# A mixture-of-experts kernel: 54 bf16 products that nothing reads are put into TensorE's stream between the last attention product and the expert stage

## What is computed

```python
# q = layernorm(x), k = v = ctx; four heads of 128
D = exp(log_D - max_log_D)                # decay from the cumulated forget gates, lower triangle
C = (q @ k.T / sqrt(dh)) * D
h = (C / (max(|C.sum|, exp(-max_log_D)) + eps)) @ v
x = x + tanh(g_xattn) * headnorm(h) * (1 + ln_weight)
xf = layernorm(x)                         # 4096 tokens
topw, topi = top_k(softmax(xf @ Wg.T), 2) # two of eight experts
# each expert takes its first CAP rows, in order of token, first choices first
y = gelu(rows @ W1[e] + b1[e]) @ W2[e] + b2[e]
x = x + tanh(g_ffn) * sum(topw * y of the two experts)
```

## Time and profile before

| | |
|---|---|
| median of 3 runs | 1940.94 us |
| lowest, highest | 1933.74, 1941.27 us |
| the profiled execution | 1937.9 us |
| its span | 1936.1 us |
| TensorE busy | 1823.9 us, 94% of the span |
| VectorE, ScalarE, GpSimd busy | 66%, 57%, 36% |
| mean granted clock of TensorE | 0.969 of full |

### The profile page before, as it was taken

How to read it: one execution, slowest core, us unless ns; L and a number is a source line. 1 busy time by engine, 2 the same in 40 slices (tenths; PEclk the granted TensorE clock), 3 DMA queues, 4 the chain that set the end, 5 groups by cost and what they waited for, 6 DMA issues and landing times.

```text
span 1936.1 us, 34120 instructions
## 1 busy us (share of the span) xinstructions
PE 1823.9 (94%) x11068; PEld 1579.1 (82%) x11068; DVE 1276.4 (66%) x2881; ACT 1107.3 (57%) x2035; POOL 688.5 (36%) x506
## 2 busy tenths in 40 slices
PE   4989977679999999999999999999999999999997
PEld 3776756578888888888888888888888888888886
DVE  3589987676667665766576657665766576657651
ACT  3567767665556555646555555555555555556543
POOL 0000110225443544354435443534354335333333
PEclk9899997589999999999999999999999999999999
DMA  5246453506554655465546555655465545554544
GB/s 172 88 170 223 152 175 109 146 18 125 105 108 92 124 99 113 90 118 99 116 86 121 99 113 93 116 99 116 91 116 96 116 94 113 98 114 90 95 72 58
DMA packets 177814, 214.77 MB, mean 111 GB/s; under 512 B 20464, under 2 KB 102512, under 8 KB 176608
## 3 DMA queue, kind: packets, MB, share of 16 engines
q0 software_dynamic: 50176, 90.77, 31.9%
q1 hardware_dynamic: 127456, 121.74, 20.1%
HBM read 123.10 MB, written 89.34 MB: 110 GB/s over the span
## 4 chain that ended last, share of the span: by engine, by line
PE 81%; DVE 7%; issue 4%; ACT 3%; DMA 2%; SPq 1%; another core or an unknown queue 0%; POOL 0%; DVEq 0%; POOLq 0%; ACTq 0%
PE PS L999 39%; PE PS L977 32%; PE PS L824 3%; DMA vs<-in_ctx_dram 2%; PE PS L815 2%; PE PS L955 2%; PE PS L763 1%; DVE x_lo L1725 1%; PE PS L888 1%; ACT heads L1110 1%; PE PS L843 1%; SPq L455 1%; DVE stats L1388 1%; DVE c_top L1746 1%; PE PS L777 1%
## 5 line engine op out<-in xcount | busy, mean ns | idle before, releaser
L677 POOL DMA_INDIRECT out_dram<-y_out,rows_now x288 | 487.5, 1693 | 828.2 <-ACT y_out L1306 687.2
L977 PE MATMUL PS<-x_hi,w_hi 128*128 128x270 f32 x1792 | 521.7, 291 | 15.0 <-issue 5.8
L977 PE MATMUL PS<-x_lo,w_hi 128*128 128x270 f32 x1792 | 517.5, 289 | 0.0
L977 PE MATMUL PS<-x_hi,w_lo 128*128 128x270 f32 x1792 | 517.1, 289 | 0.0
L999 PE MATMUL PS<-w_hi,h_hi 128*120 128x512 f32 x1152 | 458.2, 398 | 7.9 <-DVE h_lo L1732 7.9
L999 PE MATMUL PS<-w_lo,h_hi 128*120 128x512 f32 x1152 | 453.8, 394 | 0.0
L999 PE MATMUL PS<-w_hi,h_lo 128*120 128x512 f32 x1152 | 453.2, 393 | 0.0
L977 PEld LDWEIGHTS PS<-x_hi,w_hi 128*128 128x128 f32 x1792 | 340.4, 190 | 42.4 <-issue 11.8
L977 PEld LDWEIGHTS PS<-x_lo,w_hi 128*128 128x128 f32 x1792 | 341.2, 190 | 20.8
L977 PEld LDWEIGHTS PS<-x_hi,w_lo 128*128 128x128 f32 x1792 | 340.0, 190 | 0.0
L999 PEld LDWEIGHTS PS<-w_hi,h_lo 128*120 128x120 f32 x1152 | 208.9, 181 | 58.7
(11 more groups left out here) (192 smaller groups left out, 2298.6 us busy)
## 6 DMA issues: line engine op xcount, KB each, us to landing
w_raw<-in_L_ffn_W_dram SPq DMA_DIRECT2D x128, 256.0 KB, 3.8
w_raw<-in_L_ffn_W_dram SPq DMA_DIRECT2D x64, 512.0 KB
x_front<-in_x_dram SPq DMA_DIRECT2D x8, 1024.0 KB, 7.0
vs<-in_ctx_dram SPq DMA_DIRECT2D x32, 256.0 KB, 4.7
maxima<-maxima_rows SPq DMA_DIRECT2D x8, 1024.0 KB, 4.8
x_back<-in_x_dram SPq DMA_DIRECT2D x8, 1024.0 KB, 8.8
out_dram<-x_back SPq DMA_DIRECT2D x8, 1024.0 KB, 6.7
xn_rows<-xn SPq DMA_DIRECT2D x8, 1024.0 KB, 9.4
```

Of the source, the lines that this page charges most:

```text
L677: G.indirect_dma_start(out=out[:, :], out_offset=bass.IndirectOffsetOnAxis(ap=rows_now[0:RT, u % HI:u % HI + 1], axis=0), in_=y_out[0:RT, ...
L977: ins = T.matmul(product_at(k, i), w[:, slot, a, kt * P:(kt + 1) * P], v[:, side, x, kt, :], start=(kt == 0 and n == 0), stop=(kt == 1 and ...
```

## The change

One helper, `fill(n)`, issues n products of `ones_b` (128 x 128) with 512 bf16 columns of `ones` read as bf16, into bank 7, each starting anew. Nothing waits for them and nothing reads them. It is called nine times worth of FILL = 6, that is 54 products: at the start of slot B, behind an added wait for all head copies; in slot B before tables 4 to 7; at the start of slot B + 1; in slot B + 1 before the router products; after the slots before tables 8 to 11; before the last ranks; and three times FILL before TensorE waits for the table of rows.

```diff
+        FILL = 6
...
+            def fill(n):
+                for _ in range(n):
+                    T.matmul(PS[:, HEAD + 1, :], ones_b[:, :], ones[:, 0:S // 2].bitcast(BF16), start=True, stop=True)
...
             def slot(b):
                 ahead, front, last = near(b, 2), near(b, 1), near(b, -2)
                 spread = not there(b)
+                if in_slot(b, B):
+                    pe.wait_ge(head_copied, NH * B)
+                if in_slot(b, B) or in_slot(b, B + 1):
+                    fill(FILL)
                 when(b, scores, 0)
...
                 when(front, fold_gates)
+                if in_slot(b, B + 1):
+                    fill(FILL)
                 when(last, router_products)
...
                 when(last, turn_logits)
                 if in_slot(b, B):
+                    fill(FILL)
                     tables(4, 8)
...
+            fill(FILL)
             tables(8, 12)
+            fill(FILL)
             ranks(2)
             tables(12, NQ // PACK)
...
+            fill(3 * FILL)
             pe.wait_ge(table_made, 1)
             for s in range(5):
                 turn_rows(0, 0, s)
```

## The result

Over 20 runs the kernel after has a median of 1944.6 us (1938.31 to 1949.96), the kernel before one of 1940.47 us (1933.74 to 1948.71, 20 runs). The ratio is 1.0022, with a 95% interval of 1.0011 to 1.0032: slower by 4.3 us, between 2.1 and 6.2. That is within the 0.5% of the prediction's middle class, on the side and near the size that it gave (1945 us, +7.3 against the profiled execution). A second set of 12 runs of the same kernel gave 1.0026 (1.0012 to 1.0040).

The account below looks back on a forecast made before the run. Expert stage paced by TensorE at full clock, so the change acts on the seam before it: 2.6 + 2.6 + 0 + 0 + 2.6 - 0.5 = +7.3 us on 1937.9, taken as 1945; own range 1941 to 1950, with rivals 1934 to 1952.

Parts of the forecast that it names:

- Start of slot B, nothing: Start of slot B: TensorE has 5.3 us without work, a full-clock group takes 1.38 us, so 0.
- Before tables 4 to 7, +2.6: Before tables 4 to 7: no gap and a low clock, so the group costs +2.6 us; ends -1.1 and +2.6.
- nothing is absorbed at the low clock: Tables 4 to 7: ScalarE's last one-hot is ready at 339.26 us, so the 2.56 us delay passes on whole.
- the prediction's own sign of being wrong: Wrong if tables 4 to 7 run at 1.00, second expert product precedes 388.4 us, or expert stage changes over 2 us.
- Before the back turn, +2.6: Start of slot B+1, straight behind the tables: +2.6 us at low clock, bounds +0.2 and +2.6.
- Before the router products, 0 between -1.4 and +2.3: Ahead of the router: dense run brings the clock back; 0 taken, from -1.4 (up in back turns) to +2.3 (slow throughout).
- Before tables 8 to 11, 0: Before tables 8 to 11: a 1.32 us wait for ScalarE hides a fast group, 0; a slow one costs 1.24.
- Before the last ranks, +2.6: Before the last batch's ranks: no slack, +2.6 us taken; +0.3 if the tables ended early at full clock.
- Tables 14 and 15, -0.5: Tables 14 and 15: the clock may rise for them, -0.5 us taken, ends -1.1 and 0.
- The last 18, 0: Last 18 products before the gathered rows: first turn up to 2.2 us late, chain's end unmoved, 0.
- the fills never pay: Rival, chance 0.20: clock stays at 0.50 through parts 2 to 7 of the seam, +11.3 us, 1949 to 1950.
- The clock comes up and stays: Rival, chance 0.20: group before tables 4 to 7 raises the clock, later groups hold it; -4.5 us, about 1932.

Follow-up runs that it names:

- second profile: The kernel after, unchanged, profiled and run once more against the kernel before: seam 75.18 us, ratio 1.0026 (1.0012 to 1.0040).
- the kernel with only the chain groups: Kernel after, keeping only the products before tables 4 to 7, the back turn and the last ranks: ratio 1.0013 (0.9994 to 1.0031) to the kernel before.
- the kernel with products in idle places: Kernel before plus 89 products where TensorE idles: ratio 0.9991 (0.9973 to 1.0008), again 0.9980 (0.9965 to 0.9995).
- FILL 12: Kernel after with 12 products per group instead of 6: ratio to the kernel before 1.0053, again 1.0029; with zeros as moving operand 1.0048.

## Why the prediction was right

It forecast 1945, within 0.5% and on the slow side, for the reason that three of the nine groups stand on the chain at a low clock. The measured time is 1944.6, and the seam shows the reason: all three ran at the low clock in the first profile, two of them in the second. The price of one product was right: six took 2.51 to 2.56 us at the low clock and 1.29 to 1.38 at full clock, where 2.56 and 1.38 were forecast. The sum itself was too high by some 3 us, and the terms were not all right. By its own parts, from the marks (first profile after, then second, both against the first before):

1. *Start of slot B, nothing.* Right: the logits turn began 16.47 us behind the head copy in all four profiles of before and after.

2. *Before tables 4 to 7, +2.6.* The tables began 2.31 late in both. The step "nothing is absorbed at the low clock" failed. Before, the next work began 7.36 us behind the first table product; after, the third group began 6.74 behind it (337.94, 344.68) at the same low clock. The 7.44 us of the earlier trace rows were ScalarE's pace, 1.83 us a group (as in the start times of its one-hots), not TensorE's, which is 6.74 / 4 = 1.69 when all operands lie ready. So the cost was 2.31 - 0.62 = 1.7. Part 5 of the prediction has tables 8 to 11 following ScalarE at 7.45 us for four groups; part 2 did not read its own 7.44 us in the same way. In the second profile the other half failed too, that the clock stays low: with six products ahead it was up within the tables, so the prediction's own sign of being wrong was half met, and the group's cost was -0.3 (third group at 25.48, where the back turn stood at 25.76).

3. *Before the back turn, +2.6.* 2.56 in the first, 1.08 in the second.

4. *Before the router products, 0 between -1.4 and +2.3.* From the back turn to the one-hots of group 8: 10.76 before, 9.25 and 8.99 after, so -1.5 and -1.8. The clock came back, as expected, and earlier than expected, in the back turns; the low bound was the right value, even a little short. In the first profile this is the term that was mis-sized most; in the second it is part 2. In the kernel with only the chain groups, which has no products before the router, the same stretch took 8.91; so at full clock the group there costs 0.1 to 0.3.

5. *Before tables 8 to 11, 0.* From those one-hots to the ranks, less the group before the ranks, 8.0 against 8.2: -0.2. The clock fell again in these tables, as expected.

6. *Before the last ranks, +2.6.* Shown alone by its removal: 2.57.

7. *Tables 14 and 15, -0.5.* -0.2: the clock was up for tables 12 and 13 and lost in the 2.4 us wait ahead of 14.

8. *The last 18, 0.* The first turn waited 0.68 us for its rows behind them, so these products delayed nothing. From the tables' end to the first expert product it took 18.60 before and 18.91 and 20.02 after. The kernel without those 18 products (chain groups only) took 19.66, so they are not shown to be the reason; the gathers' landing differs by that much.

First profile: 4.25 - 1.51 + 2.35 - 0.16 + 0.31 = 5.24. Second: 0.80 - 1.77 + 2.34 - 0.15 + 1.42 = 2.64. The forecast's 7.3 had 5.2, 0, 2.6, -0.5 and 0 in these places. What came behind the seam (+0.75 to +2.6 us between the profiles) is in none of the parts, and no run shows why it came.

The level was right in part by luck: the sum was laid on the profiled 1937.9, and the typical time before is 1940.5; too low a start and too high a sum gave 1945. A sum of 4 on the median would have been the better working.

Of the rivals, "the fills never pay" was refuted by the router run at 1.00. "The clock comes up and stays" did not happen in the kernel after, but the second profile had its first half, and the kernel with products in idle places had all of it once. The Trainium skill's rule ("TensorE: Matmul & The Clock Gate", section "Why this matters for your kernels"), that unbroken matmul work brings the full clock and idle gaps take it away, was half borne out: idle gaps took it (the 2.4 us ahead of table 14), unbroken table products at the low clock did not bring it (6.80 busy of 6.80 us at 0.50), and table products with long bf16 rows among them kept it in one profile (to 57.4 us) and lost it in another (at 37.5).

Two readings of the prediction were too narrow. It has the clock raised by "bf16 streams" at 349.5 us, but 1.6 of the 3.5 us before were the router's fp32 products. And in the kernel before, fp32 transposes of 128 columns alone, behind 7.8 us of waiting, were followed by full clock:

```profile
48.94 3.74 PE L763 MATMUL PS<-ident,vs 128*128 128x128 f32 x16 [7.83 <-DMA vs<-in_ctx_dram]
```

```profile
48.94:52.50 3.56, 3.56 (x17) 3.20 (x18) 0.30 (x3) 1.76 (x3) 0.00 (x0) 0.50 0.00 0
52.50:56.00 3.50, 3.50 (x25) 2.89 (x25) 0.12 (x1) 3.18 (x8) 0.63 (x1) 1.00 0.00 0
```

So full clock has also followed work that was neither bf16 nor 512 columns wide.

## What to carry to other kernels

A product that only keeps the clock up is free where TensorE waits at the clock that it will then have, and costs its duration wherever the chain passes; so look first for which waits exist, and whether the engine behind them is paced by another, since then a faster clock gives nothing back. Tables of 7.4 us at the low clock that could halve to 3.7 at full clock are worth nothing when ScalarE feeds them at 1.83 us a group (the back turn at 25.77 against 25.76). And compare such kernels by marks inside the trace, from the last common event, in more than one profile: the same kernel moved by 2.6 us in its seam and by 4.4 us ahead of it from one execution to the next.

## What the runs showed of the hardware beside this

The same six products ahead of tables 4 to 7 (2.5 us at the low clock) were followed by full clock at 22.8 us behind the last head copy in one execution of the kernel after and at 30.5 in the other; the kernels with the same group and other groups left out had 22.4 and 29.9. Twelve (5.0 us) were followed by it at 23.0 to 23.5 in all three profiles, with zeros as with ones. Short fp32 work, tables and the turns around them, did not raise the clock in 14 us (13.33 us busy). Table products did not lose it either when they ran without pauses: with twelve products ahead, tables 4 to 7 ran at full clock to their end (3.7 us). With ScalarE's pauses between them it was lost in tables 8 to 11 in the kernel after, and held there in the first profile of FILL 12.
